# A graph network's set-up in five pieces beside the first builds, and node degrees taken per batch

## What is computed

```python
def conv(h, W, b):                     # W is (2*64 + 16, 64)
    m = concatenate([h[dst], h[src], edge_attr], axis=1) @ W + b
    return segment_sum(m, dst, num_segments=12500)
h = relu(conv(x, W1, b1))
h = relu(conv(h, W2, b2))
out = layernorm(x + conv(h, W3, b3))
```

## Time and profile before

| | us |
|---|---|
| median of 3 runs | 3054.26 (3053.72 to 3057.09) |
| the profiled execution | 3058.39 |
| its span, first to last instruction | 3056.6 |
| PE busy | 2773.0 (91%) |
| DVE busy | 1580.2 (52%) |
| ACT busy | 1260.1 (41%) |
| POOL busy | 2176.2 (71%) |

### The profile page before, as it was taken

One profiled execution on the slowest core, in us unless ns is written; L12 is line 12 of the kernel. 1 busy time (PEld: TensorE's weight loads), 2 busy tenths in 40 slices (PEclk: granted clock), 3 DMA queues, 4 the chain that ended last, 5 costly groups with the idle time before them and its releaser, 6 DMA issues.

```text
span 3056.6 us, 59532 instructions
## 1 busy us (share of the span) xinstructions
PE 2773.0 (91%) x22952; PEld 1737.1 (57%) x22952; DVE 1580.2 (52%) x3129; ACT 1260.1 (41%) x2314; POOL 2176.2 (71%) x2168
## 2 busy tenths in 40 slices
PE   0049999999999999999968999999998999999998
PEld 0015656565655566565545666666665666666665
DVE  6378999999999999999611111111111111211211
ACT  1049888889898888888500000000000000000000
POOL 2734877787878778787738878777755877877773
PEclk9988999999999999999989999999999999999999
DMA  2143444453535353544586999888888799988882
GB/s 54 34 86 119 127 126 141 115 152 102 162 103 164 103 162 106 158 110 146 164 200 164 214 214 213 218 205 214 213 207 197 182 210 214 209 215 206 215 204 60
DMA packets 248448, 489.58 MB, mean 160 GB/s; under 512 B 161870, under 2 KB 197545, under 8 KB 220045
## 3 DMA queue, kind: packets, MB, share of 16 engines
q1 hardware_dynamic: 141766, 272.31, 33.7%
q10 hardware_dynamic: 58404, 143.10, 17.2%
q0 software_dynamic: 48000, 70.35, 11.9%
HBM read 341.83 MB, written 143.70 MB: 159 GB/s over the span
## 4 chain that ended last, share of the span: by engine, by line
PE 63%; DVE 22%; POOL 8%; issue 4%; ACT 2%; DMA 1%; SPq 0%; ACTq 0%; POOLq 0%; DVEq 0%
PE ps L1099 29%; PE ps L1107 16%; DVE is_key L916 9%; PE ps L1080 6%; DVE is_low L906 4%; POOL far_rows L677 4%; PE ps L1131 3%; PE ps L1160 3%; DVE masks L924 2%; POOL blocks L663 2%; ACT blocks L753 2%; PE ps L1161 2%; DVE far_masks L939 2%; PE ps L1121 2%; PE ps L1135 1%
## 5 line engine op out<-in xcount | busy, mean ns | idle before, releaser
L677 POOL DMA_INDIRECT far_rows<-parts,far_src x1350 | 1481.0, 1097 | 517.2 <-issue 378.0
L1099 PE MATMUL ps<-blocks,parts 125*128 125x375 fp8e4 x7500 | 1544.7, 324 | 3.8 <-ACT blocks L753 2.1
L753 ACT ACTIVATE blocks<-ps 125x505 fp8e4<-125x505 f32 x1875 | 1111.5, 787 | 141.8 <-PE ps L1080 141.8
L1099 PEld LDWEIGHTS ps<-blocks,parts 125*128 125x128 bf16 x7500 | 740.5, 100 | 421.7 <-issue 19.8
L1080 PE MATMUL ps<-is_key,is_low 128*125 128x505 bf16 x1875 | 720.5, 393 | 29.6 <-DVE is_key L916 14.2
L916 DVE TENSOR_SCALAR is_key<-from_one,parts 128x500 bf16<-128x500 f16 x1875 | 696.0, 419 | 25.7 <-PE ps L1080 19.7
L1107 PE MATMUL ps<-blocks,parts 125*64 125x375 fp8e4 x7500 | 685.8, 326 | 0.0
L1107 PEld LDWEIGHTS ps<-blocks,parts 125*64 125x64 bf16 x7500 | 398.5, 110 | 275.0 <-issue 154.1
L976 DVE COPY z<-ps 125x256 f32<-125x256 f32 x75 | 31.5, 420 | 899.1 <-PE ps L1161 862.4
L1080 PEld LDWEIGHTS ps<-is_key,is_low 128*125 128x125 bf16 x1875 | 257.7, 138 | 258.6 <-DVE is_key L916 100.9
L939 DVE SCALAR_TENSOR_TENSOR far_masks<-far_dst,from_one 128x2250 fp8e4<-128x2250 int32 x75 | 187.7, 2502 | 325.3 <-PE ps L1135 321.0
(11 more groups left out here) (102 smaller groups left out, 1521.0 us busy)
## 6 DMA issues: line engine op xcount, KB each, us to landing
blocks<-counts SPq DMA_DIRECT2D x100, 1066.4 KB
counts<-blocks ACTq DMA_DIRECT2D x25, 4101.6 KB
blocks<-counts SPq DMA_DIRECT2D x100, 984.4 KB
far_rows<-parts,far_src POOLq DMA_INDIRECT x1350
blocks<-counts SPq DMA_DIRECT2D x100, 123.8 KB
counts<-blocks ACTq DMA_DIRECT2D x25, 476.1 KB
blocks<-counts SPq DMA_DIRECT2D x100, 114.3 KB
attr_stage<-in_edge_attr SPq DMA_DIRECT2D x125, 88.0 KB
```

What stands on the lines that cost most here:

```text
L677: nc.gpsimd.indirect_dma_start(far_rows[:, g % 2, j, :], None, parts_d[layer], bass.IndirectOffsetOnAxis(ap=far_src[:, g % BATCHES, j:j + ...
L753: nc.scalar.activation(blocks[0:L, b % 2, :, n * W:(n + 1) * W], build[0:L, c % BUILD, 0:COLS].rearrange("p (t w) -> p t w", w=W), ACT.Cop ...
L1099: nc.tensor.matmul(acc_ps(g), parts[0:L, layer % 2, t, 0:2, :].rearrange("p k d -> p (k d)"), blocks[0:L, g % 2, t, :], start=(t == 0), st ...
```

## The change

- Table: ScalarE copies the spread table from PSUM to SBUF (table_rows); find_bases counts there.
- Lists: only the 375 dense targets of a batch have chunks now. There are 15 lists in 5 pieces (PIECES) of 3 (PIECE); piece i holds the chunks of batches 5i to 5i+4. One more list of 25 rows is for the starts of the far groups.
- Gathers: one of dst and one of src for each list, 256 edges wide from the place in the table, in place of 128 edges at the table's place and 128 at the exact start. Where an edge of the chunk lies in the first 128, copy_predicated takes it from there (sort_out).
- Order: bases of pieces 0 to 2 and sort_out(0) stand ahead of the first build; the rest (set_up) stands in VectorE's queue between the chunks of batch 0: bases at n = 0 and 4, the x split at 1 and 10, sort_out at 16, 24, 32, 40, give_starts at 41, place_groups at 60. turn_keys (TensorE) and keep_keys (ScalarE) follow at the same n. The store of the x parts (SP) stands ahead of that of the starts.
- Degrees: from the attribute sums, whose last row is a sum of ones. turn_deg (four small matmuls) after unit 0, keep_deg at n=12, scale_rows at n=20. keep_h moves to n=32, make_nodes to 68, make_rows to 73, turn_h to the end of unit 2, conv to units 4 to 7. SP's loads of the next h and far_src move from k=1 to k=3.
- find_bad also compares the number of edges found in the chunks with that of the degrees.

The diff, cut to its core:

```diff
-    LISTS = ALL_CHUNKS // L
...
+    PIECES = 5
+    SPAN = BATCHES // PIECES
+    RUN = L // SPAN
+    PIECE = BUILDS // RUN
+    LISTS = PIECES * PIECE
...
+    PIECE_AT = [0, 16, 24, 32, 40]
...
-            sp.dma_start(x_stage, x.rearrange("(t p) d -> p t d", p=L)).then_inc(x_staged, DMA)
+            for t in range(T):
+                sp.dma_start(x_stage[:, :, t, :], x.rearrange("(b t p) d -> p b t d", p=L, t=T)[:, :, t, :]
+                             ).then_inc(x_staged, DMA)
...
+            sp.wait_ge(x_split, 1)
...
+                sp.dma_start(x_table[rows, :, :], parts[rows, 0, :, :, :].rearrange("p t a d -> p t (a d)")
+                             ).then_inc(parts_stored[0], DMA)
...
-                sp.dma_start(starts_d.rearrange("(k p) -> p k", p=L), starts).then_inc(starts_stored, DMA)
-                sp.wait_ge(starts_stored, DMA)
...
+                sp.dma_start(starts_d.rearrange("(p k) -> p k", k=LISTS), starts[:, 0:LISTS]).then_inc(starts_stored, DMA)
+                sp.dma_start(far_starts_d.rearrange("(b a) -> b a", a=1), starts[0:BATCHES, LISTS:LISTS + 1]
+                             ).then_inc(starts_stored, DMA)
+                sp.wait_ge(starts_stored, 2 * DMA)
+                for k in range(NEAR):
+                    l, run = divmod(k * GROUP_CHUNKS, RUN)
+                    sp.dma_start(group_row[:, :, :, k],
+                                 starts_d.rearrange("(a b r i l) -> a i b r l", a=1, b=SPAN, r=RUN, l=PIECE)[:, :, :, run, l]
+                                 ).then_inc(start_row_loaded, DMA)
+                sp.dma_start(group_row[:, :, :, NEAR], far_starts_d.rearrange("(a i b) -> a i b", a=1, b=SPAN)
                              ).then_inc(start_row_loaded, DMA)
-                sp.wait_ge(deg_ready, 1)
-                sp.dma_start(deg_d.rearrange("(k p r) -> p k r", p=L, r=W), deg_chunk).then_inc(deg_stored, DMA)
-            sp.wait_ge(deg_stored, DMA)
-            sp.dma_start(deg_rows, deg_d.rearrange("(t l) -> t l", l=L)).then_inc(deg_loaded, DMA)
...
-                        elif k == 1 and g + 1 < BATCHES:
+                        elif k == 3 and g + 1 < BATCHES:
...
                                     base=0, pattern=[[-1, P]], channel_multiplier=1).then_inc(consts_ready, 1)
...
-                for k in range(LISTS):
-                    nc.gpsimd.indirect_dma_start(
-                        into[:, k, :], None, one_by_one(edges),
-                        bass.IndirectOffsetOnAxis(ap=start_ints[:, k:k + 1], axis=0)).then_inc(landed, DMA)
+                    into[0:rows, k, :], None, one_by_one(edges),
+                    bass.IndirectOffsetOnAxis(ap=base_ints[0:rows, k:k + 1], axis=0)).then_inc(landed, DMA)
+            for i in range(PIECES):
+                pool.wait_ge(bases_ready, i + 1)
+                for k in range(i * PIECE, (i + 1) * PIECE):
+                    gather_window(dst, dst_w, k, L, dst_landed[i])
+                for k in range(i * PIECE, (i + 1) * PIECE):
+                    gather_window(src, src_w, k, L, src_landed[i])
+            gather_window(dst, dst_w, LISTS, BATCHES, far_window_landed)
             def gather_rows(g, j):
                 layer = g // BATCHES
...
-            act.wait_ge(x_split, 1)
+            act.wait_ge(table_spread, 1)
+            nc.scalar.copy(table_rows.rearrange("p (q c) -> p q c", q=4), table_ps).then_inc(table_kept, 1)
...
+                return parts[0:L, 0, :, part, :].rearrange("p (b t) d -> p b t d", t=T)
+            def keep_keys(i):
...
+                    act.wait_ge(keys_turned, 2 * i + which + 1)
+                    nc.scalar.copy(into[:, i * SPAN:(i + 1) * SPAN, :].rearrange("p b (l r) -> p l b r", r=RUN),
+                                   ps[:, 6 + which, 0:PIECE * L].rearrange("p (l b r) -> p l b r", l=PIECE, b=SPAN)
+                                   ).then_inc(keys_kept, 1)
+            keep_keys(0)
+            act.wait_ge(x_staged, T * DMA)
+            nc.scalar.copy(x_part(0), x_stage).then_inc(x_hi, 1)
             def keep_counts(b, n):
                 c = b * BUILDS + n
+                if n == 0 and b == 1:
+                    act.wait_ge(starts_stored, 2 * DMA)
                 if n == 0 and b >= 2:
...
@@ -764,8 +790,7 @@
             def scale_rows(b):
                 act.wait_ge(h_loaded[b % 2], (b // 2 + 1) * 2 * DMA)
...
+                act.wait_ge(deg_kept, b + 1)
                 for t in range(T):
...
                 for n in range(BUILDS):
+                    if g == -1:
+                        if n == 4:
+                            act.wait_ge(x_left, 1)
+                            nc.scalar.copy(x_part(1), x_stage).then_inc(x_mid, 1)
+                        elif n and n in PIECE_AT:
+                            keep_keys(PIECE_AT.index(n))
+                    if g >= 1 and n == 20:
+                        scale_rows(g - 1)
                     if g + 1 < BATCHES:
                         keep_counts(g + 1, n)
-                    if g >= 0 and n == 54:
-                        scale_rows(g)
-                    if g >= 1 and n == 60:
...
+            dve.wait_ge(table_kept, 1)
+            def find_bases(lists, rows):
+                for k in lists:
+                    last = nc.vector.tensor_scalar(below[0:rows, :], table_rows[0:rows, :], first_node[0:rows, k:k + 1], 0.0,
+                                                   ALU.is_lt, ALU.add, accum_out=coarse[0:rows, k:k + 1])
+                    ordered(last)
+                at = coarse[0:rows, lists[0]:lists[-1] + 1]
+                ordered(nc.vector.tensor_scalar(at, at, float(P), float(-P), ALU.mult, ALU.add))
+                ordered(nc.vector.tensor_scalar(at, at, 0.0, float(E - 2 * P), ALU.max, ALU.min))
+                return nc.vector.tensor_copy(base_ints[0:rows, lists[0]:lists[-1] + 1], at)
...
+            def piece_bases(i):
+                find_bases(range(i * PIECE, (i + 1) * PIECE), L).then_inc(bases_ready, 1)
...
+            def find_starts(rows, lists):
+                mask = reached[0:rows, 0:lists.stop - lists.start, :]
+                ordered(nc.vector.tensor_tensor(mask, dst_w[0:rows, lists, :], firsts(rows, lists, 2 * P), ALU.is_ge))
+                ordered(nc.vector.tensor_reduce(rest_of[0:rows, lists], mask, axis=X, op=ALU.add))
...
+            def sort_out(i):
+                lists = slice(i * PIECE, (i + 1) * PIECE)
+                dve.wait_ge(dst_landed[i], PIECE * DMA)
+                find_starts(L, lists)
+                dve.wait_ge(src_landed[i], PIECE * DMA)
+                in_first = reached[:, :, 0:P]
+                ordered(nc.vector.copy_predicated(dst_w[:, lists, P:2 * P], in_first, dst_w[:, lists, 0:P]))
+                ordered(nc.vector.copy_predicated(src_w[:, lists, P:2 * P], in_first, src_w[:, lists, 0:P]))
+                dst_of, src_of = dst_w[:, lists, P:2 * P], src_w[:, lists, P:2 * P]
+                rel, low_of = dst_of.bitcast(fp32), src_of.bitcast(fp32)
+                valid, tile_of = dst_w[:, lists, 0:P].bitcast(fp32), src_w[:, lists, 0:P].bitcast(fp32)
+                nc.vector.tensor_tensor(rel, dst_of, firsts(L, lists, P), ALU.subtract)
+                ordered(nc.vector.tensor_scalar(tile_of, src_of, 1.0 / L, -0.496, ALU.mult, ALU.add))
+                nc.vector.tensor_scalar(valid, rel, 0.0, None, ALU.is_ge)
+                ordered(nc.vector.tensor_scalar(tile_of, tile_of, ROUND, None, ALU.add))
+                nc.vector.scalar_tensor_tensor(out=valid, in0=rel, scalar=float(W), in1=valid, op0=ALU.is_lt, op1=ALU.mult)
+                ordered(nc.vector.tensor_scalar(tile_of, tile_of, ROUND, None, ALU.subtract))
+                nc.vector.tensor_reduce(found_of[:, lists], valid, axis=X, op=ALU.add)
+                nc.vector.scalar_tensor_tensor(out=rel, in0=tile_of, scalar=float(W), in1=rel, op0=ALU.mult, op1=ALU.add)
+                ordered(nc.vector.scalar_tensor_tensor(out=low_of, in0=tile_of, scalar=float(-L), in1=src_of, op0=ALU.mult, op1=ALU.add))
+                nc.vector.tensor_scalar(low_of, low_of, 1.0, None, ALU.add)
+                nc.vector.scalar_tensor_tensor(out=rel, in0=rel, scalar=1.0, in1=valid, op0=ALU.add, op1=ALU.mult
+                                               ).then_inc(keys_made, 1)
...
+            def give_starts():
+                lists = slice(LISTS, LISTS + 1)
+                dve.wait_ge(far_window_landed, DMA)
+                find_starts(BATCHES, lists)
+                ordered(nc.vector.scalar_tensor_tensor(out=starts[:, 0:LISTS], in0=coarse[:, 0:LISTS], scalar=float(2 * P),
+                                                       in1=rest_of[:, 0:LISTS], op0=ALU.add, op1=ALU.subtract))
+                nc.vector.scalar_tensor_tensor(out=starts[0:BATCHES, lists], in0=coarse[0:BATCHES, lists], scalar=float(2 * P),
+                                               in1=rest_of[0:BATCHES, lists], op0=ALU.add, op1=ALU.subtract
```

(96 more changed lines are left out.)

215 lines of the change are left out of this document (78 added, 137 removed).

## The result

The changed kernel takes **3035.43 us** (median of 10 runs, 3026.0 to 3049.86) against 3057.78 (10 runs, 3053.72 to 3065.38) on the same chips: ratio 0.9925, 95% interval 0.9913 to 0.9937. It is faster by 0.75%, where 2980 us (2.4%) was forecast with a range of 2950 to 3012. The profiled execution took 3026.32 us, 32.1 less than that of before.

What follows compares the result with a forecast made beforehand. The prediction saw a set-up relay of waits, then TensorE and VectorE both near full in layer 0, then TensorE alone. From 3054.3 us, -96.6 (set-up) + 21.6 (batches) + 0.9 = -74.1 gave 2980, range 2950 to 3012.

Steps and rivals of the forecast that it cites:

- Set-up: Everything before the first apply matmul: it would begin near 151 us instead of 247.58, a gain of 96.6 us.
- rival 3: Set-up: find_bases reading SBUF blocks POOL's gathers; 2976 us at double rate, 2990 at single rate; chance 0.06.
- turn_deg 0.87: End of unit 0 in each layer-0 batch: the new degree matmuls hold TensorE for 0.87 us.
- wait before turn_h 0.65: End of unit 2 in each layer-0 batch: TensorE waits 0.65 us for ScalarE's scaled rows.
- 1.2 at build 62: Layer-0 batch: TensorE is 1.2 us later at build 62, from 0.87 + 0.65 - 0.35.
- keep_h's move: VectorE's queue, n=11 to 32: leaves the place ahead of build 13; half its 0.68 us, 0.35, given back.
- the two waits of before: Before builds 65 and 66: waits of 0.22 and 0.54 us go, giving back 1.15 with their overhang.
- Build 73, which waited 0.30 before, waits about 1.4: Late in each layer-0 batch: nodes (about 2.1 us) and far_masks (about 2.5) fall between keys 68 and 73.
- the 24 batches: Layer-0 batches: each grows by 0.9 us, from 52.07 to 53.0, a loss of 21.6 us in all.
- Rival 2: Layer-0 batches lose 2.0 us each: turn_h wait and nodes/far_masks crowding add up, nothing given back; 3006 us, chance 0.20.
- Rival 1: Layer-0 batches lose nothing, as TensorE's new work falls into waits it has anyway; 2958 us, chance 0.15.
- Rival 4's ring: Layer-0 batches: four hand-overs close a ring of engines waiting on each other; slower than before, 3066 us at 4.5 each; chance 0.04.

Runs made afterwards that it cites:

- e4: Changed kernel with the four degree matmuls of turn_deg issued twice in each batch: 3054.45 us, ratio 0.9988.
- e10: e1 with ScalarE's four scalings moved from before eviction 20 to before eviction 18: 2948.03 us, ratio 0.9654.
- e12: e10 with the far masks made after key 74 instead of before key 72 (ahead of key 73): 2951.39 us, ratio 0.9649.
- e9: Changed kernel with twelve more wide matmuls (375 columns) on TensorE ahead of build 73: 3006.46 us, ratio 0.9842.
- e6: e1 with the degree matmuls of turn_deg issued twice in each batch, as in e4: 2977.64 us, ratio 0.9738.
- e2: Kernel before with only make_nodes moved from n=53 to 68 and make_rows from 60 to 73: 3112.75 us, ratio 1.0173.
- e3: Changed kernel with make_nodes at n=63 instead of 68, make_rows staying at 73: 3004.59 us, ratio 0.9818.
- e1: Changed kernel with the node update put a batch later, into VectorE's idle stretch before keep_acc, make_rows behind it: 2959.46 us, ratio 0.9677.
- e5: Changed kernel with a ring of seven key buffers instead of six: 3033.81 us, ratio 0.9926.

## Why the prediction was off

**Set-up: right** in sum (-97.85 for -96.6) and by its terms. Only the x subtractions blocked POOL (gathers of 6.94 and 7.85 us, ending 1.1 us behind them), as the earlier trace rows showed; the passes from SBUF at 1.95 blocked nothing, so rival 3 did not come. The Trainium skill (SBUF — State Buffer, who interferes with whom) leaves the accumulating form of tensor_scalar out of the operations that take the shared port pair; the trace agrees.

**turn_deg 0.87, wait before turn_h 0.65, 1.2 at build 62: right in size, in part by luck.** They measured 0.87 (e4), 0.68 and 1.06. But 0.30 of the wait stood there before too, so only 0.38 is new (and e10 gives back 0.36), where the forecast counted 0.65 as new; its own rows give 0.5 to 0.6 for it. By difference keep_h's move gave back 0.2 and not 0.35, and the two errors nearly cancel. At build 66 the two waits of before had been won back, as written (0.05 was forecast there, -0.10 measured).

**"Build 73, which waited 0.30 before, waits about 1.4": the step that failed, as a mis-sized term.** The place and the cause are as put. The size was 0.47 before build 70 and 2.08 before build 73; with the small ones 3.0, as TensorE takes 5.2 us from build 68 to build 73 (1124.20 to 1129.41) and 2.2 where no key is late (e12). A sum over the stretch gives it: from the end of key 68 to that of key 73 VectorE needs 7.1 us, 1.9 for the nodes, 2.4 for the far masks and 2.8 for five keys with their is_low; TensorE's own work is 2.2, and VectorE's lead at key 68 is 2.0. The difference is 2.9. The prediction names only the two big items for this stretch and shows no working for the 1.4; the keys' own time, 2.3 by the earlier trace rows, stands nowhere in it. Against the kernel before, which had short stands there too, the forecast adds 0.7 from build 66 to build 74; build 66 comes 0.1 earlier and build 74 2.4 later, so it is 2.5. A batch without a stretch takes 54.26 instead of 53.0: 1.8 more here, some 0.5 less in the other terms together.

**A price that was in no term: the clock.** The forecast let a stand cost its own length. Here it costs 1.0 a batch more (55.28 against e9's 54.26), 23 us of the traced 23 batches and 29 of the medians. In the kernel before, the longest stand for a key was 0.6 us, and no batch but the last had such a stretch. The runs of the changed kernel spread over 24 us and e9's over 5; but e6's spread over 18 with no stretch in its trace, so the clock isn't shown to be the reason for that.

**The sum.** Forecast -74.1 for the span, measured -32.2: set-up -97.9 instead of -96.6, the first batch -1.2, the 24 batches +76.2 instead of +21.6 (of the 55 more, some 31 by the crowding, 23 by the clock, 1 in the last batch), what follows layer 0 -9.4 instead of +0.9. This last was in no term. POOL's first gather of layer 1 comes 24.1 us after the last keep_acc instead of 36.4. In all 14 traces the rest of the run goes with this gather: it lasts 1508 to 1510 us from the last keep_acc where the gather comes at 22 to 26 us, 1511 to 1513 at 29 to 31, 1517 to 1518 at 36 to 38. The kernel before with late nodes (e2) is in the middle group (29.2) and the changed kernel with the update at 63 (e3) in the last (37.5), so it isn't the set-up; why the gather comes earlier or later stays open.

**The rivals.** Rival 2 named the failing place, the crowding of nodes and far masks, at 2.0 a batch and 3006 us; without the clock the batches lose 2.2 (e9: 3006.46), and the clock makes the rest. That the number fits is in part luck: rival 2 had nothing given back, and the waits at builds 65 and 66 were given back, while the crowding is 2.5 against the kernel before. The range ended at 3012 since nothing in it could cost more than its own duration. Rival 1 is false: TensorE's new work doesn't fall into waits that it has anyway (e4, e6: 0.8 to 0.9 of 0.87 stays on the path). e1 has batches of 51.94 and ends at 2959.5, near rival 1's 2958, since the new work, +1.06 at build 62, is won back at builds 65 and 66 by the forecast's own term. Rival 4's ring did not close; what couples TensorE and VectorE is the limit of keys and is_low ahead (e4, e5).

## What to carry to other kernels

When steps are moved in the queue of an engine that feeds another through a short ring, lay all of its work between two hand-overs (the routine pieces too) against what the consumer does in that stretch plus the lead at its start. Put such steps where the engine stands anyway, not where it is merely ahead: the 2 us of the node update cost 76 us more ahead of key 69 than in the idle stretch, some 23 of them by the clock. And look at the granted clock around each new stand of TensorE; here a stand of 2 us cost another 1.0 us a batch on the mean.

## What was not expected of the hardware

- From the end of a stand of 2.08 us on TensorE ran at half clock (0.50) for 3.4 or 6.8 us in 11 of 23 batches. The Trainium skill (TensorE: Matmul & The Clock Gate, the HAM clock gate) says that the clock follows how busy the array has been; the trace agrees. With eight instructions of one column in the stand (1.03 us, 1.12 of stand left) there were 15 such stretches, with twelve of 375 columns (2.07 us, 0.17 left) none.
- Extra matmuls in a stand made a kernel 29 us faster (e9).
- An indirect gather 256 edges wide held POOL 1.20 us, the same as one 128 wide.
- A VectorE operation with two SBUF inputs of 6400 columns held POOL's gather until 1.1 us behind its own end: 6.9 and 7.9 us instead of 1.2.
